# Who scales the exponentials: moving the softmax normalisation from VectorE to GpSimd in two attention layers

## The reference

```python
def _L1_xattn_ref(hidden_states, cross_attention_states, attention_mask, Wq, Wk, Wv, Wo, q_norm_w, k_norm_w):
    ...
    scores = jnp.einsum('bhqd,bhkd->bhqk', q, k) * scale
    scores = scores + attention_mask[:, :, :, :kv_len]
    probs = jax.nn.softmax(scores.astype(jnp.float32), axis=-1).astype(q.dtype)
    out = jnp.einsum('bhqk,bhkd->bhqd', probs, v)
    out = out.transpose(0, 2, 1, 3).reshape(bsz, q_len, H * HD)
    return out @ Wo.T
```

## Time and profile before

| what | us |
|---|---|
| three executions, median (lowest to highest) | 2835.53 (2832.22 to 2836.23) |
| the profiled execution, its own time | 2840.14 |
| its span from first to last instruction | 2838.3 |
| PE busy | 2559.7 (90%) |
| DVE busy | 1461.0 (51%) |
| ACT busy | 828.4 (29%) |
| POOL busy | 413.5 (15%) |
| the layer 0 attention runs from about | 840 to 1380 |
| the layer 1 attention runs from about | 1615 to 2635 |

### The profile page before, as it was taken

One profiled execution on the slowest core, in us unless ns is written; L12 is line 12 of the kernel. 1 busy time (PEld: TensorE's weight loads), 2 busy tenths in 40 slices (PEclk: granted clock), 3 DMA queues, 4 the chain that ended last, 5 costly groups with the idle time before them and its releaser, 6 DMA issues. The chain is left out here.

```text
span 2838.3 us, 32291 instructions
## 1 busy us (share of the span) xinstructions
PE 2559.7 (90%) x12384; PEld 2114.8 (75%) x12384; DVE 1461.0 (51%) x2473; ACT 828.4 (29%) x1922; POOL 413.5 (15%) x285
## 2 busy tenths in 40 slices
PE   8999999799988899998779699999999999999824
PEld 6888888689975677776569467888888888887723
DVE  6222222223003666666443446666666666666697
ACT  3222222223112333333200233333333333333323
POOL 3000000000001112111021112222222222221020
PEclk9999999899997999999889899999999999999766
DMA  6222221242231222221021123232222323322001
GB/s 193 67 67 71 67 75 60 87 171 85 74 110 56 70 70 76 78 68 49 17 72 33 58 65 93 81 100 90 92 95 87 101 83 99 96 79 75 6 0 47
DMA packets 159354, 217.38 MB, mean 77 GB/s; under 512 B 31510, under 2 KB 124082, under 8 KB 158178
## 3 DMA queue, kind: packets, MB, share of 16 engines
q1 hardware_dynamic: 159202, 215.33, 24.8%
HBM read 176.99 MB, written 38.29 MB: 76 GB/s over the span
## 5 line engine op out<-in xcount | busy, mean ns | idle before, releaser
L1025 POOL TENSOR_TENSOR attend_w_hi<-attend_w_raw,attend_one 128x1024 fp32r<-128x1024 f32 (+1 forms) x184 | 336.8, 1832 | 1209.1 <-DMA attend_w_raw<-in_wo 968.6
L1291 PE MATMUL attend_ps_score<-attend_k_in,attend_q 128*100 128x361 f32 (+1 forms) x768 | 303.1, 518 | 26.8 <-ACT attend_p L1044 25.6
L1237 PE MATMUL attend_ps_gemm<-attend_o_hi,attend_w_hi 128*128 128x400 f32 x704 | 293.5, 417 | 37.0 <-DVE attend_w_lo L1122 29.2
L1237 PE MATMUL attend_ps_gemm<-normed_hi,attend_w_hi 128*128 128x400 f32 x704 | 268.0, 381 | 38.8 <-DVE attend_w_lo L1122 38.8
L1122 DVE TENSOR_TENSOR attend_w_lo<-attend_w_raw,attend_w_hi 128x1024 fp32r<-128x1024 f32 (+1 forms) x184 | 213.6, 1194 | 151.9 <-POOL attend_w_hi L1025 150.9
L1237 PE MATMUL attend_ps_gemm<-attend_o_hi,attend_w_lo 128*128 128x400 f32 x704 | 246.8, 351 | 0.0
L1237 PE MATMUL attend_ps_gemm<-attend_o_lo,attend_w_hi 128*128 128x400 f32 x704 | 246.7, 350 | 0.0
L1237 PE MATMUL attend_ps_gemm<-normed_lo,attend_w_hi 128*128 128x400 f32 x704 | 244.2, 347 | 0.0
L1237 PE MATMUL attend_ps_gemm<-normed_hi,attend_w_lo 128*128 128x400 f32 x704 | 243.1, 345 | 0.0
L1047 ACT ACTIVATE attend_p<-attend_p,attend_neg_max 100x361 f32<-100x361 f32 x256 | 150.7, 590 | 308.1 <-DVE attend_neg_max L1147 308.1
L1311 PE MATMUL attend_ps_out<-attend_pt,attend_v_in 121*128 121x400 f32 (+4 forms) x640 | 235.8, 506 | 1.0 <-ACT attend_pt L1084 1.0
(11 more groups left out here) (247 smaller groups left out, 4889.2 us busy)
## 6 DMA issues: line engine op xcount, KB each, us to landing
attend_w_raw<-in_wq SPq DMA_DIRECT2D x88, 512.0 KB, 4.6
attend_w_raw<-in_wo SPq DMA_DIRECT2D x64, 512.0 KB, 3.6
attend_w_raw<-in_wo SPq DMA_DIRECT2D x32, 384.0 KB, 3.2
context_ctx_raw<-in_ctxT SPq DMA_DIRECT2D x8, 1456.0 KB
attend_k_in<-scratch_k SPq DMA_DIRECT2D x64, 180.5 KB
context_ctx_raw<-in_ctxF SPq DMA_DIRECT2D x22, 512.0 KB, 4.7
scratch_v<-context_v_out SPq DMA_DIRECT2D x44, 256.0 KB, 2.2
scratch_k<-context_kt_out SPq DMA_DIRECT2D x44, 256.0 KB, 5.1
```

The costliest lines, as they stand in the source:

```text
L1025: pool.tensor_tensor(hi, w_flat(w_raw, j % RAW, j), one[:hi.shape[0]].to_broadcast(hi.shape), ALU.mult).then_inc(w_hi_done, 1)
L1237: mm = pe.matmul(out, left[a](c), right[b](c), start=(c == 0 and a == b == 0), stop=(c == chunks - 1 and a == 1))
L1291: pe.matmul(ps_score[:S, h % 2, :NK], q[:, i % 2, h, k * S:(k + 1) * S], k_in[:, u % KV_SLOTS], start=True, stop=True).then_inc(s_done, 1)
```

## The change: what it does

The four products of a unit leave DVE. POOL makes them, each as a `tensor_tensor` of the head's exponentials with the reciprocal broadcast along the keys. DVE keeps the reciprocal (its helper is now called `invert`). POOL's order is now written step by step: first the roundings of the first tiles and of step 0, then the products of unit 0, and then in each step `u` the roundings of the tiles of step `u + 1` and behind them the products of unit `u + 1`. DVE's reciprocal has one wait more, so that it does not overwrite one that POOL still reads.

```diff
@@ gpsimd
-            for j in range(len(tiles)):
+
+            def weights(j):
                 pool.wait_ge(w_load[j % RAW], (j // RAW + 1) * 16)
                 if j >= SPLIT:
                     kind, n = tiles[j - SPLIT]
...
                 hi = w_flat(w_hi, j % SPLIT, j)
                 pool.tensor_tensor(hi, w_flat(w_raw, j % RAW, j), one[:hi.shape[0]].to_broadcast(hi.shape), ALU.mult
                                    ).then_inc(w_hi_done, 1)
+
+            def normalise(u):
+                if u >= NU:
+                    return
+                slot = u % P_SLOTS
+                pool.wait_ge(inverted, u + 1)
+                for h in range(HG):
+                    pool.tensor_tensor(p[:, slot, h], p[:, slot, h], exp_inv[:, slot, h:h + 1].to_broadcast([S, NK]), ALU.mult
+                                       ).then_inc(p_ready, 1)
+
+            for j in range(LEAD):
+                weights(j)
+            for j in step_tiles(0):
+                weights(j)
+            normalise(0)
+            for u in range(NU):
+                for j in step_tiles(u + 1):
+                    weights(j)
+                normalise(u + 1)
@@ vector
-            def normalise(u):
+            def invert(u):
                 if u >= NU:
                     return
                 slot = u % P_SLOTS
                 dve.wait_ge(exped, (u + 1) * HG)
+                if u >= P_SLOTS:
+                    dve.wait_ge(p_ready, (u - P_SLOTS + 1) * HG)
                 dve.reciprocal(exp_inv[:, slot], exp_sum[:, slot]).then_inc(inverted, 1)
-                dve.wait_ge(inverted, u + 1)
-                for h in range(HG):
-                    dve.tensor_scalar(p[:, slot, h], p[:, slot, h], exp_inv[:, slot, h:h + 1], None, ALU.mult
-                                      ).then_inc(p_ready, 1)
...
-            normalise(0)
+            invert(0)
...
-                normalise(u + 1)
+                invert(u + 1)
```

## The result

The changed kernel takes 2864.96 us (median of four runs, 2858.25 to 2870.44) against 2835.73 before (2832.22 to 2836.23). The ratio is 1.0105 with a 95% interval of 1.0082 to 1.0128: 1.05% slower, 3.0 us above the forecast of 2862 and inside its range. The profiled execution took 2864.31 us, its span is 2862.5, 24.2 us longer than that of before.

A forecast was written before the change was run, and what follows sets the result against it. PE was taken to bound both attentions, so only delays of its next instruction counted. Terms of 9.7 us in layer 0 and 17.0 in layer 1 gave +26.7 on the 2835.5 median: 2862 us, range 2849 to 2882.

The forecast's parts named there:

- Side and place: Slower by more than 0.2%, chance 0.89; loss in first units and after steps without query, steps with a query unchanged.
- Rival 2: No exclusion between POOL's products and DVE's splits, so only late heads count: +15.8 us, 2851 us; chance 0.13.
- rival 3: Faster: DVE without the products begins o_lo and split earlier, PE's w_lo waits vanish: 15.5 us less, 2820; chance 0.04.
- rival 4: No difference: PE's delays vanish in later waits, 2835.5 us; chance 0.07.
- Price of a product: POOL's product per head: 0.87 us for 361 columns, 1.01 for 461; low end 0.78 and 0.95, high 1.00 and 1.28.
- The first units: First unit of each layer: nothing hides POOL's slower products, +2.5 us in layer 0 and +2.1 in layer 1.
- Layer 1, units 59 to 61: Split runs before the fourth product, whose transposition comes 3.25 us late; PE absorbs 0.16: 3 x 3.1 = +9.3 us.
- Layer 0, units 25 to 31: The rounding, now behind the products, holds the split PE waits for: +0.99 us each, 7 x 1.0 = +6.9 us.
- units 9 and 17: Layer 0, units 5, 9, 13, 17, 21: PE 1.96 us late, all taken by existing waits, so 0.
- The wait of 1.09 us in unit 5: Layer 0: PE's wait for ACT, set by DVE's order, takes the 0.67 us left after the w_lo wait.
- The loads behind a split that is held start up to 0.9 us later: Steps with a query: free, as the last rounding ends 2.35 us before the reciprocal.

The follow-up runs named there:

- experiment 1: The changed kernel with the products of bare units (no query projection ahead of them) back on DVE: 2828.86 us, ratio 0.9973 to the kernel before.
- experiment 2: The changed kernel with POOL making products only in bare units (no query projection ahead), DVE all others: 2868.93 us, ratio 1.0116 to the kernel before.
- experiment 3: The kernel before, with POOL's query-tile rounding waiting for DVE's first exponential bias in layer 0's steps 4, 8, 12, 16, 20: 2831.33 us, ratio 0.9974.
- experiment 6: The changed kernel with DVE's reciprocal made early in the step and layer 0's exponential bias on ACT: 2828.81 us, ratio 0.9974 to the kernel before.
- experiment 7: The changed kernel with POOL rounding the next step's tile ahead of the products in steps of one tile: 2861.12 us, ratio 1.0086 to the kernel before.
- experiment 9: The changed kernel with POOL's product written as tensor_scalar instead of tensor_tensor: 2989.67 us, ratio 1.0545 to the kernel before.
- experiment 12: The kernel before with the split ahead of o_lo, bias on ACT and POOL's products in units behind a query projection: 2794.36 us, ratio 0.9865.
- experiment 8: The changed kernel with PE waiting once for all four products of a unit instead of head by head: 2871.09 us, ratio 1.0114 to the kernel before.
- experiment 5: The changed kernel with DVE's reciprocal made early, right behind its first copy of the step: 2849.52 us, ratio 1.0045 to the kernel before.

## Why the prediction was right, and where it was not

- **Side and place: right, and the mechanism in kind.** DVE's time became a wait (137.8 us, forecast about 140). Units 4 to 57 of layer 1 did not change. The loss is in the bare units, as experiments 1 and 2 show. Rival 2 (no exclusion) falls with the split of 1.85 us, rival 3's mechanism (DVE relieved) with experiments 3 and 6, rival 4 with the 1.05%.
- **Price of a product: too high.** The term took 0.87 and 1.01 us, between rows; 0.744 and 0.912 were measured, just under the low end. The first units lost 2.2 and 1.7 us up to the fourth head, forecast 2.5 and 2.1.
- **Layer 1, units 59 to 61: the largest term, 9.3 us, was right in its late heads and wrong in the hold.** The step "third product until 2567.57, split next, fourth product until 2569.61" rests on the third product ending behind the split's arrival at 2.33 us; at 0.744 the fourth had begun at 2.29, and was not held. The split was, but PE did not wait for it. A late unit of layer 1 costs 1.28 us at equal clock, not 3.1, and all of it is late heads. So rival 2's path, not the forecast's, gave the time of these units, though its premise (no exclusion) is false.
- **Layer 0, units 25 to 31: the stall too high, too.** The term was +0.99 each by the held split. At equal clock it was +0.46, and experiment 7 puts only 0.35 of it on the late rounding.
- **No term for the clock.** This is what made good most of the above. Of the +9.2 us in units 25 to 30 of layer 0 some 6.5 are above six times 0.46, of the +7.9 in layer 1's units 60 to 62 some 4.1 above three times 1.28, and the +1.7 of units 5, 13 and 21 of layer 0 came at 0.91, where units 9 and 17 gave 0 at 1.00, as forecast. So about 12 us of the sum are TensorE's slower clock behind the new waits, and I had priced every wait as its length.
- **No term for the gain.** It was worth 0.26%, 7 to 8 us. The wait of 1.09 us in unit 5 was read rightly: the bias ahead of it took 0.17 us, and units 9 and 13 have the same wait. But PE's waits for ACT in steps 4, 8, 12 and 20 (1.32 us in step 8) had no term at all, and those were set by a bias held by a rounding. Rows 8 had the exclusion, but I looked for it on large instructions only. And "The loads behind a split that is held start up to 0.9 us later", priced as free, had the right fact and no look at what the later rounding would no longer meet.
- **The sum.** +26.7 forecast, +29.2 measured between the medians, by terms that erred by up to 12 us in both directions. The time was right in good part by luck: terms that were too high, a clock that had no term, and a gain that had none cancelled.

## What to carry to other kernels

A new lateness costs its length at the engine that bounds, plus what that engine's clock loses behind it; here the second was about as large as the first (some 12 us against 13, counted from the periods and the first units' heads). When an instruction is moved between two engines that exclude each other, list every instruction of the one that can meet the other, the tiniest first: one of 0.17 us, held to 1.7, cost 1.5 us a step, a split of 1.0 us held to 1.4 cost 0.35, and a split of 1.2 us held to 1.85 cost nothing where PE came later anyway. When a set of instructions takes longer than expected, look at them one by one before calling it their price: one of four had stood for another engine (experiment 9). And when an engine waits in every step, look at what stands behind the wait: putting it ahead gave 1.1%, as much as the whole change had cost.

## What the runs showed of the hardware

- A DVE `tensor_scalar` on 100x2, 0.17 us alone, that begins while POOL rounds a 128x1024 tile (1.89 us) ends when the rounding ends: begun 0.30, 0.24 and 0.89 us behind the rounding's start (steps 4, 8 and 9 of before) it took 1.61, 1.68 and 1.03 us, 1.91 or 1.92 in sum each time. In the trace of before 16 of 64 took 0.45 us or more, the longest 1.89, and 14.8 us more than their 0.17 in all. Where it began 0.16 us ahead of the rounding, it took 0.17 and the rounding its 1.89.
- POOL's `tensor_scalar` with a scalar for each partition takes 1.17 us for 361 columns and 1.42 for 461, its `tensor_tensor` with the same scalar broadcast 0.744 and 0.912 (experiment 9 and the change). Against DVE's splits the two forms behave differently. Of `tensor_tensor` products and splits, queued together, each waits for one of the other (experiment 12, 1.7 to 1.8 us each). A `tensor_scalar` product that met two splits stood for both (3.22 us instead of 1.19). In layer 0, 25 splits of 0.96 us began 0.24 us behind such a product's start and took 1.22 us, while the product kept its 1.44: these two ran side by side for most of their time. The page "SBUF — State Buffer" of the Trainium skill (section "Who interferes with whom") says that a DVE instruction with two SBUF inputs contends with a GpSimd instruction that reads SBUF. Layer 1 agrees by the 3.22 us; layer 0 agrees only in part, by the 0.26 us that a split lost. Why the two could overlap there stays open.
- TensorE's clock fell to its lower level behind one to three units in a row that waited 1.1 us or so for POOL's heads (the change, experiments 2 and 7; with one longer wait instead, experiment 8). It stayed at 1.00 in units 9 and 17 of the change, which had the same waits, and in experiment 5, whose units 25 to 29 took 13.21 us against 12.86 in units 25 and 26 of the change, with the added wait ahead of the scores. Which property of the waits decides was not found.
